# Attention stage of a transformer block: probabilities left unscaled, one query block's probabilities turned by way of DRAM, scores in plain fp32

## The chip, the cores and the metric

The kernel runs on one NeuronCore of one Trainium2 chip. The metric is the device time of one launch in microseconds; the number reported is the median of the runs.

## The reference

The input is 8192 tokens of width 512. It is layer-normalised to `xn`, and the output is `x + attention(xn) + feed_forward(xn)`. What matters here is the attention: 16 heads of width 32, in windows. A block of 128 queries sees three blocks of keys (its own and its two neighbours), masked to a distance of at most 128 tokens.

```python
qkv = (x @ Wqkv + bqkv)                      # q, k, v of 16 heads, 32 wide
scores = einsum('bhnqd,bhnkd->bhnqk', qb, kwin) * scale
attn   = softmax(where(mask, scores, -1e30)) # 128 queries x 384 keys
out    = einsum('bhnqk,bhnkd->bhnqd', attn, vwin)
return out @ Wout + bout
```

## The kernel before

There are two stages. The first, the feed-forward stage (up to about 1131 us), is not touched; it leaves the normalised input, transposed and split into a high and a low part, in DRAM. The second is `attention_stage`. Products whose operands are split run as three passes in the round fp32r form (high by high, low by high, high by low).

The attention stage has 128 steps `t` (`STEPS`). Step `t = 4 i + c` treats the two query blocks of token pair `i` (b = 0 and b = 1) for the four heads of channel group `c`. A query block of one head is a 128 x 384 tile of scores. Engines run their queues in the order in which the code writes them, and meet only at semaphores. Per step:

- TensorE (lines from 1064): `scores(t,0)`: three passes for four heads, 32 contraction rows for each head, one strip of the array for each (L1176). Then four quarters, each `turn_probs(t-1, 1, h)` (three 128 x 128 transposes, L1193) and a quarter of job A, which projects queries and keys for step t+2 (`run_a`, 24 matmuls of 256 columns, L1105). Then `scores(t,1)`, then `probs_times_values(t-1)` (L1217, plain fp32, four heads in four column strips of 32). Then four quarters, each `turn_probs(t, 0, h)` and a quarter of job B (`run_b`, 12 matmuls of 512 columns, L1114 for values or L1123 for the output projection).
- VectorE: `find_max` (L1006) adds the mask, scales and takes the maximum while it moves scores from PSUM to `probs`; `normalise` takes the reciprocal of the sums (L1017) and scales the probabilities of three heads of four (L1021); `qk_low` makes the low parts of queries and keys (L1034, L1038); `oT_low` (L1027) that of the product with the values; `add_out` (L1048) the output.
- ScalarE: `exp` (L928, with the sum and an accumulator read), `copy_pT` (L938, transposed probabilities from PSUM to SBUF), the high parts (L946, L954, L957), `take_v` (L921).
- GpSimd: the scaling of the fourth head (L888), key copies, `add_bias` (L899).
- SyncE's queue issues every DMA: `load_x` (L840), `load_part` (L846), `store_y` (L850), in one order written out by hand. It waits in that order too.

So before, all eight 128 x 384 tiles of a step are scaled and then turned by TensorE, 24 transposes in a step. The two `job_ps` banks are used in turn, and `wait_job_bank` holds a job until the job two before it was read out.

Of the kernel before, what the change touches and what calls it, by code (L numbers as in the profile page):

```python
# [22 lines left out]
P = 128  # L23
# [638 lines left out]
def attention_stage(nc, loaded, xT_dram, partial, out):  # L662
# [6 lines left out]
    VR = 6  # L669
    XR = 3  # L670

    ctx = ExitStack()
    with ctx:
# [18 lines left out]
        q_hi = sb("q_hi", [P, DC, 2, P], F32R)  # L692
        q_lo = sb("q_lo", [P, DC, 2, P], F32R)
        k_hi = sb("k_hi", [P, DC, 6, P], F32R)
        k_lo = sb("k_lo", [P, DC, 6, P], F32R)
# [5 lines left out]
        pT = wqkv_raw[:, 2:4, :].rearrange("p a (h w k) -> p (a h) w k", w=6, k=P)  # L701
        oT_hi = sb("oT_hi", [P, 2, DC, T], F32R)
        oT_lo = sb("oT_lo", [P, 2, DC, T], F32R)
# [13 lines left out]
        k0_hi, k0_done = sem("k0_hi"), sem("k0_done")  # L717
        qk_hi_done, qk_done = sem("qk_hi_done"), sem("qk_done")
# [6 lines left out]
        normalised, last_head_normalised = sem("normalised"), sem("last_head_normalised")  # L725
# [3 lines left out]
        oT_hi_done, oT_done = sem("oT_hi_done"), sem("oT_done")  # L729
# [40 lines left out]

        def job_a(t):
            return t + 2 if t + 2 < STEPS else None
# [19 lines left out]
        def job_release(n):  # L792

            t, k = divmod(n, 3)
            if k == 0:
                return (qk_done, job_a(t) + 1) if job_a(t) is not None else None
            if k == 1:
                return (oT_done, t) if 1 <= t <= STEPS else None
            b = job_b(t)
            if b is None:  # L800
                return None
            return (v_done, 2 * b[1] + b[2] + 2) if b[0] == "v" else (out_added, 2 * b[1] + b[2] + 1)

        def wait_job_bank(pe, n):
# [4 lines left out]
            if n >= 0:  # L809
                pe.wait_ge(*job_release(n))  # L810
            elif n % 2 == 0:
                pe.wait_ge(v_done, 2)
            else:
                pe.wait_ge(qk_done, 2)
# [17 lines left out]
        def _(sp):  # L832
# [14 lines left out]

            def store_y(i, b):
# [8 lines left out]
            for i in range(NT + 1):  # L857
                if 1 <= i:
                    for b in range(2):
                        store_y(i - 1, b)  # L860
                        if i < NT:
                            load_part(i, b)
                if i + XR - 1 < NT:
                    load_x(i + XR - 1)
            for b in range(2):
                sp.wait_ge(y_stored[b], 16 * NT)

        @block.gpsimd
        def _(pool):
# [13 lines left out]
            def normalise_last_head(t, b):  # L883
                i, _ = where(t)
                cols = window(i, b)
                u = b * HC + HC - 1
                pool.wait_ge(rcp_done, 2 * (2 * t + b) + 2)
                nc.gpsimd.tensor_scalar(probs[:, u, cols], probs[:, u, cols], sum_rcp[:, u:u + 1], None, ALU.mult  # L888
                                        ).then_inc(last_head_normalised, 1)

            def copy_keys(u):
                i, c = where(u)
                pool.wait_ge(qk_done, u + 1)
                nc.gpsimd.tensor_copy(k_hi[:, c, 0:2, :], k_hi[:, c, 4:6, :])
                nc.gpsimd.tensor_copy(k_lo[:, c, 0:2, :], k_lo[:, c, 4:6, :]).then_inc(keys_copied, 1)
# [7 lines left out]
            for t in range(STEPS + 3):  # L903
# [3 lines left out]
                if t < STEPS:  # L907
                    normalise_last_head(t, 0)
                if job_a(t) is not None and where(job_a(t))[0] % 2 == 0:
                    copy_keys(job_a(t))  # L910
                if t < STEPS:
                    normalise_last_head(t, 1)
# [3 lines left out]
        def _(act):  # L916
            def take_v(i, r, number, bank):
                act.wait_ge(job_filled, number)
                if i >= 2:
                    act.wait_ge(pv_done, 4 * i - 4)  # L920
# [10 lines left out]
            def copy_pT(t, b, h):  # L931
                i, _ = where(t)
                seen = blocks_seen(i, b)
                first = 3 * at(i, b)
                act.wait_ge(turned, 8 * t + b * HC + h + 1)
                if t >= 1:
                    act.wait_ge(pv_done, t)
                nc.scalar.copy(pT[:, h, first + seen.start:first + seen.stop, :].rearrange("p w t -> p (w t)"),  # L938
                               pT_ps[:, h % 2, seen.start * P:seen.stop * P]).then_inc(pT_done, 1)

            def oT_high(t):
                i, c = where(t)
                act.wait_ge(pv_done, t + 1)
                if i >= 2 and c == 0:
                    act.wait_ge(job_filled, B_NUMBER[4 * (i - 1) + 2])
                nc.scalar.copy(oT_hi[:, i % 2, c, :], job_ps[:, pv_bank(t), 0:T]).then_inc(oT_hi_done, 1)  # L946

            def qk_high(u, number, bank):
# [3 lines left out]
                if u >= DC:  # L952
                    act.wait_ge(scored, 2 * (u - DC) + 2)
                nc.scalar.activation(q_hi[:, c, :, :].rearrange("p b t -> p (b t)"), job_ps[:, bank, 0:T], ACT.Identity,  # L954
                                     bias=qk_bias[:, c:c + 1], scale=1.0)
                half = new_keys_at(i)
                nc.scalar.activation(k_hi[:, c, half:half + 2, :].rearrange("p b t -> p (b t)"),  # L957
                                     job_ps[:, bank, T:2 * T], ACT.Identity,
                                     bias=qk_bias[:, DC + c:DC + c + 1], scale=1.0).then_inc(qk_hi_done, 1)
# [9 lines left out]
            for c in range(DC):  # L969
                last = nc.scalar.activation(k_hi[:, c, keys_start(0) + 1, :], job_ps[:, 0, c * P:(c + 1) * P], ACT.Identity,  # L970
                                            bias=qk_bias[:, DC + c:DC + c + 1], scale=1.0)
            last.then_inc(k0_hi, 1)
            take_v(-1, 1, 2, 1)
            for u in range(2):
                qk_high(u, 3 + u, u)
            take_v(0, 0, 5, 0)
            for t in range(STEPS + 3):
# [3 lines left out]
                for h in range(HC):  # L981
                    if 1 <= t <= STEPS:
                        copy_pT(t - 1, 1, h)
                    if t < STEPS:
                        exp(t, 0, h)
                if job_a(t) is not None:
                    qk_high(job_a(t), A_NUMBER[t], a_bank(t))
                for h in range(HC):
                    if t < STEPS:
                        exp(t, 1, h)  # L990
                    if h == 0 and 1 <= t <= STEPS:
                        oT_high(t - 1)
                    if t < STEPS:
                        copy_pT(t, 0, h)

        @block.vector
        def _(dve):
            def find_max(t, b):
# [3 lines left out]
                if t >= 1:  # L1002
                    dve.wait_ge(turned, 8 * (t - 1) + HC * (b + 1))
# [6 lines left out]
            def normalise(t, b):  # L1010
                i, _ = where(t)
                cols = window(i, b)
                for pair in range(2):
                    first = b * HC + 2 * pair
                    heads = slice(first, first + 2)
                    dve.wait_ge(exped, 8 * t + first + 2)
                    nc.vector.reciprocal(sum_rcp[:, heads], prob_sum[:, heads]).then_inc(rcp_done, 1)  # L1017
                    dve.wait_ge(rcp_done, 2 * (2 * t + b) + pair + 1)
                    for u in range(first, first + 2):
                        if u % HC < HC - 1:  # L1020
                            nc.vector.tensor_scalar(probs[:, u, cols], probs[:, u, cols], sum_rcp[:, u:u + 1], None,  # L1021
                                                    ALU.mult).then_inc(normalised, 1)

            def oT_low(t):
                i, c = where(t)
                dve.wait_ge(oT_hi_done, t + 1)
                nc.vector.tensor_tensor(oT_lo[:, i % 2, c, :], job_ps[:, pv_bank(t), 0:T],  # L1027
                                        oT_hi[:, i % 2, c, :].bitcast(F32), ALU.subtract).then_inc(oT_done, 1)

            def qk_low(u, bank):  # L1030
                i, c = where(u)
                half = new_keys_at(i)
                dve.wait_ge(qk_hi_done, u + 1)
# [319 lines left out]
```

## Time and profile before

| | us |
|---|---|
| median of 3 runs | 2630.59 (2626.28 to 2631.04) |
| profiled execution | 2629.41, span 2627.6 |
| TensorE matmul busy | 2576.2 (98%) |
| ScalarE / VectorE / GpSimd busy | 1638.1 / 1592.0 / 631.8 |
| mean granted TensorE clock | 0.989 |
| HBM traffic | 97.43 MB read, 67.11 MB written |

The span is the time from the first to the last instruction; what a run takes beyond it (1.8 us here) lies around it. Busy shares are means over both stages. In the chain of waits each piece is work that nothing could have started earlier; its sum is the span.

### The profile page before, as it was taken

The page shows a single profiled execution, that of the slowest core. Times are in us where ns is not written, and L with a number is a line of the kernel's source. Part 1 is how long each engine was busy: PE and PEld are TensorE (multiplying, and loading weights), DVE is VectorE, ACT ScalarE, POOL GpSimd, SP SyncE. Part 2 cuts the span into 40 slices and gives each one's busy share as a digit, 9 for nine tenths or more (in the row PEclk, how much of TensorE's full clock was granted, in tenths as well). Part 3 has the DMA queues.
Part 4 walks back from the last instruction along what each step waited for, and adds up shares of the span by engine and source line. Part 5 has one row for each costly group of instructions (what it writes and reads, how often), then busy time and mean ns, then how long its engine had stood idle before and what let it go on. Part 6 is the DMA issues. An engine that isn't in the chain of part 4 may idle for free.

```text
span 2627.6 us, 55989 instructions
## 1 busy us (share of the span) xinstructions
PE 2576.2 (98%) x19728; PEld 2090.2 (80%) x19728; DVE 1592.0 (61%) x4779; ACT 1638.1 (62%) x4260; POOL 631.8 (24%) x595
## 2 busy tenths in 40 slices
PE   6999999999999999989999999999999999999998
PEld 4888888888888888868888888888888888888885
DVE  5444444444444444357777777777777777777775
ACT  6333333333333333358888888888888888888886
POOL 0011111111111111033333333333333333333332
PEclk7999999999999999999999999999999999999999
DMA  5422222222222222021121111112111111112110
GB/s 181 146 80 81 80 80 80 80 80 80 80 80 80 80 80 64 33 81 34 34 65 34 53 46 42 58 41 58 34 61 39 42 58 42 58 34 65 34 46 29
DMA packets 188361, 167.43 MB, mean 64 GB/s; under 512 B 11328, under 2 KB 143424, under 8 KB 187632
## 3 DMA queue, kind: packets, MB, share of 16 engines
q1 hardware_dynamic: 188000, 164.41, 20.2%
q8 instruction: 132, 2.16, 0.4%
q14 instruction: 85, 0.70, 0.1%
q0 software_dynamic: 144, 0.17, 0.0%
HBM read 97.43 MB, written 67.11 MB: 63 GB/s over the span
## 4 chain that ended last, share of the span: by engine, by line
PE 55%; ACT 1%; issue 0%; DVE 0%; POOL 0%; POOLq 0%; ACTq 0%
PE pT_ps L1193 14%; PE job_ps L1105 14%; PE score_ps L1176 7%; PE job_ps L1123 7%; PE job_ps L1217 7%; PE job_ps L1114 7%; ACT wqkv_raw L928 1%; ACT wqkv_raw L938 0%; PE job_ps L1237 0%; PE score_ps L1227 0%; DVE wqkv_raw L1006 0%; DVE k_lo L1038 0%; ACT q_hi L954 0%; ACT k_hi L957 0%; POOL wout_raw L899 0%
## 5 line engine op out<-in xcount | busy, mean ns | idle before, releaser
L928 ACT ACTIVATE wqkv_raw<-wqkv_raw,neg_max 128x384 f32<-128x384 f32 (+1 forms) x1024 | 633.3, 619 | 186.3 <-DVE neg_max L1006 181.5
L888 POOL TENSOR_SCALAR wqkv_raw<-wqkv_raw,sum_rcp 128x384 f32<-128x384 f32 (+1 forms) x256 | 372.9, 1457 | 960.1 <-DVE sum_rcp L1017 960.1
L494 ACT ACTIVATE relu<-up_ps,fc_scale 128x512 f32<-128x512 f32 x256 | 176.2, 688 | 656.2 <-PE up_ps L625 656.2
L938 ACT COPY wqkv_raw<-pT_ps 128x384 f32<-128x384 f32 (+1 forms) x1024 | 484.7, 474 | 74.4 <-PE pT_ps L1193 74.1
L1193 PE MATMUL pT_ps<-ident,wqkv_raw 128*128 128x128 f32 x3040 | 513.4, 277 | 8.1 <-ACT wqkv_raw L938 7.7
L1006 DVE CUSTOM_DVE_ANT_0 wqkv_raw<-score_ps,mask 128x384 f32<-128x384 f32 (+1 forms) x1024 | 503.5, 548 | 5.7 <-PE score_ps L1176 1.6
L568 DVE SCALAR_TENSOR_TENSOR sq<-up_ps,relu 128x512 f32<-128x512 f32 x256 | 177.0, 692 | 531.8 <-ACT relu L494 530.4
L1193 PEld LDWEIGHTS pT_ps<-ident,wqkv_raw 128*128 128x128 f32 x3040 | 360.0, 140 | 119.1 <-ACT wqkv_raw L938 42.6
L635 PE MATMUL down_ps<-proj_T,sq_hi 128*128 128x512 f32 x1024 | 408.9, 399 | 0.9 <-DVE sq_lo L551 0.9
L637 PE MATMUL down_ps<-proj_T,sq_lo 128*128 128x512 f32 x1024 | 404.3, 395 | 0.0
L621 PE MATMUL up_ps<-f_xT_hi,fc_T 128*128 128x512 f32 x1024 | 399.2, 390 | 1.4 <-DVE low L539 1.4
L623 PE MATMUL up_ps<-f_xT_lo,fc_T 128*128 128x512 f32 x1024 | 399.2, 390 | 0.0
L1105 PE MATMUL job_ps<-xT_hi,wqkv_hi 128*128 128x256 f32 x1024 | 329.0, 321 | 0.1
L1021 DVE TENSOR_SCALAR wqkv_raw<-wqkv_raw,sum_rcp 128x384 f32<-128x384 f32 (+1 forms) x768 | 298.2, 416 | 17.9
L1017 DVE RECIPROCAL sum_rcp<-prob_sum 128x2 f32<-128x2 f32 x512 | 85.0, 166 | 354.5 <-ACT wqkv_raw L928 354.0
L1105 PE MATMUL job_ps<-xT_hi,wqkv_lo 128*128 128x256 f32 x1024 | 287.9, 281 | 0.0
L1105 PE MATMUL job_ps<-xT_lo,wqkv_hi 128*128 128x256 f32 x1024 | 287.8, 281 | 0.0
L454 POOL TENSOR_TENSOR f_y<-f_y,part_in 128x512 f32<-128x512 f32 x64 | 86.9, 1389 | 665.1 <-DVE f_y L559 665.1
L635 PEld LDWEIGHTS down_ps<-proj_T,sq_hi 128*128 128x128 f32 x1024 | 193.4, 189 | 43.9 <-DVE sq_lo L551 2.2
L621 PEld LDWEIGHTS up_ps<-f_xT_hi,fc_T 128*128 128x128 f32 x1024 | 192.3, 188 | 44.0 <-DVE low L539 2.2
L637 PEld LDWEIGHTS down_ps<-proj_T,sq_lo 128*128 128x128 f32 x1024 | 193.0, 188 | 43.0
L623 PEld LDWEIGHTS up_ps<-f_xT_lo,fc_T 128*128 128x128 f32 x1024 | 192.3, 188 | 42.5
(126 smaller groups left out, 4228.2 us busy)
## 6 DMA issues: line engine op xcount, KB each, us to landing
xT_hi<-xT SPq DMA_DIRECT2D x65, 256.0 KB, 3.8
xT_lo<-xT SPq DMA_DIRECT2D x65, 256.0 KB, 4.5
f_x_in<-in_L_attn_x SPq DMA_DIRECT2D x64, 256.0 KB, 3.2
xT<-f_xT_hi SPq DMA_DIRECT2D x64, 256.0 KB, 2.6
xT<-f_xT_lo SPq DMA_DIRECT2D x64, 256.0 KB, 2.8
part_in<-in_L_attn_x SPq DMA_DIRECT2D x64, 256.0 KB, 3.4
partial<-f_y SPq DMA_DIRECT2D x64, 256.0 KB, 2.0
wout_raw<-partial SPq DMA_DIRECT2D x64, 256.0 KB, 2.8
```

The source lines that it names most:

```text
L621: nc.tensor.matmul(up_ps[:, s % 2, :], fc_T[:, k, cols], xT_hi[:, par, k, :], start=(k == 0), stop=False)
L623: nc.tensor.matmul(up_ps[:, s % 2, :], fc_T[:, k, cols], xT_lo[:, par, k, :], start=False, stop=False)
L635: nc.tensor.matmul(down_ps[:, b, :], sq_hi[:, s % 2, t], proj_T[:, s, :], start=(s == 0), stop=False)
L637: last = nc.tensor.matmul(down_ps[:, b, :], sq_lo[:, s % 2, t], proj_T[:, s, :], start=False, stop=(s == FB - 1))
L888: nc.gpsimd.tensor_scalar(probs[:, u, cols], probs[:, u, cols], sum_rcp[:, u:u + 1], None, ALU.mult).then_inc(last_head_normalised, 1)
L928: nc.scalar.activation(probs[:, u, cols], probs[:, u, cols], ACT.Exp, bias=neg_max[:, u:u + 1], scale=-1.0, accum_out=prob_sum[:, u:u + 1] ...
L938: nc.scalar.copy(pT[:, h, first + seen.start:first + seen.stop, :].rearrange("p w t -> p (w t)"), pT_ps[:, h % 2, seen.start * P:seen.stop ...
L1006: nc.vector.tensor_tensor_reduce(out=probs[:, u, cols], in0=score_ps[:, h, cols], in1=mask[:, cols], scale=-SCORE_SCALE, scalar=3e38, op0= ...
L1021: nc.vector.tensor_scalar(probs[:, u, cols], probs[:, u, cols], sum_rcp[:, u:u + 1], None, ALU.mult).then_inc(normalised, 1)
L1105: last = nc.tensor.matmul(job_ps[:, bank, is_k * T:(is_k + 1) * T], w[:, k, col:col + P], tokens, start=(m == 0), stop=(m == PASSES * DC - 1))
L1114: last = nc.tensor.matmul(job_ps[:, bank, :], a[:, k, x_slot(i) + r, :], w[:, k, 2 * D:3 * D], start=(n == 0), stop=(n == PASSES * DC - 1))
L1193: last = nc.tensor.transpose(pT_ps[:, h % 2, w * P:(w + 1) * P], probs[:, u, w * P:(w + 1) * P], ident[:, :])
```

## The change

Four things change together, all in the attention stage.

1. Probabilities stay unscaled. `inverse_sums` takes one reciprocal for four heads; GpSimd widens it to 32 columns for each head (`rcp_wide`); TensorE turns it (one transpose more in two of the four `turn_probs`), and `scale_oT` multiplies the product with the values by it, once for a step.
2. The probabilities of query block b = 0 are no longer turned by TensorE. VectorE turns 32 x 32 squares (`turn_blocks`), one DMA writes the four heads to DRAM (`move_blocks_out`, 786,432 bytes in pieces of 512 bytes) and four DMAs read them back in turned order (`move_blocks_in`). `probs_times_values` waits for that.
3. The product with the values is issued as six blocks of 128 columns for each head, instead of two of 256 and two of 128.
4. Scores are one plain fp32 product for each head, instead of three fp32r passes. Queries and keys are no longer split: `take_q` (ScalarE) and `take_k` (VectorE).

The values ring goes from 6 to 5 slots; the split product ring becomes `OR = 6` slots of one step. The bank of a product is released by `oT_scaled`, earlier by `oT_done`. The diff, cut to its core ("..." marks what is left out):

```diff
+        queries = sb("queries", [P, DC, 2, P], F32)
+        keys = sb("keys", [P, DC, 6, P], F32)
+        blocks = wqkv_raw[:, 3, :].rearrange("p (a w h t) -> p a w h t", w=3, h=HC, t=DH)
+        pT_moved = wqkv_raw[:, 2, :].rearrange("p (w q h t) -> p w q h t", q=STRIPS, h=HC, t=DH)
+        pT = sb("pT", [P, HC, 4, P], F32)
+        rcp_wide = sb("rcp_wide", [P, 2, HC, DH], F32)
...
             if k == 1:
-                return (oT_done, t) if 1 <= t <= STEPS else None
+                return (oT_scaled, t) if 1 <= t <= STEPS else None
...
+            def move_blocks_out(t):
+                sp.wait_ge(blocks_turned, HC * (t + 1))
+                if first == 0:
+                    sp.dma_start(moved.rearrange("a w p x -> p (a w) x"),
+                                 blocks.rearrange("p a w h t -> p (a w) (h t)")).then_inc(blocks_out, 16)
...
+            def move_blocks_in(t):
+                sp.wait_ge(blocks_out, 16 * transfers_out(t + 1))
+                if t >= 1:
+                    sp.wait_ge(pv_done, t)
+                for a in range(STRIPS):
+                    moved = turned_dram[t % 2 * STRIPS + a, first:3, :, :].rearrange("w (q j) x -> j (w q) x", j=DH)
+                    sp.dma_start(pT_moved[a * DH:(a + 1) * DH, first:3, :, :, :].rearrange("j w q h t -> j (w q) (h t)"),
+                                 moved).then_inc(blocks_moved, 16)
...
+            for t in range(STEPS + DC):
+                i, c = where(t)
+                if t < STEPS:
+                    move_blocks_out(t)
+                    move_blocks_in(t)
+                if c == 1 and i + XR - 1 < NT:
                     load_x(i + XR - 1)
+                if c >= 2 and i >= 1:
+                    store_y(i - 1, c - 2)
+                    if i < NT:
+                        load_part(i, c - 2)
...
                 for h in range(HC):
                     if 1 <= t <= STEPS:
-                        copy_pT(t - 1, 1, h)
+                        copy_pT(t - 1, h)
                     if t < STEPS:
                         exp(t, 0, h)
-                    qk_high(job_a(t), A_NUMBER[t], a_bank(t))
+                    take_q(job_a(t), A_NUMBER[t], a_bank(t))
                 for h in range(HC):
                         exp(t, 1, h)
-                    if h == 0 and 1 <= t <= STEPS:
-                        oT_high(t - 1)
-                    if t < STEPS:
-                        copy_pT(t, 0, h)
+                if 1 <= t <= STEPS:
+                    oT_high(t - 1)
...
+            def turn_blocks(t, u):
+                dve.wait_ge(exped, 8 * t + u + 1)
+                if u == 0 and t >= 1:
+                    dve.wait_ge(blocks_out, 16 * transfers_out(t))
+                nc.vector.transpose(blocks[:, :, seen.start:seen.stop, u, :].rearrange("p a w t -> p w a t"),
+                                    probs[:, u, seen.start * P:seen.stop * P].rearrange("p (w a t) -> p w a t", a=STRIPS, t=DH)
+                                    ).then_inc(blocks_turned, 1)
+
+            def scale_oT(t):
+                dve.wait_ge(pv_done, t + 1)
+                if t >= 1:
+                    dve.wait_ge(oT_done, t)
+                nc.vector.tensor_tensor(oT.rearrange("p (b t) -> p b t", t=P),
+                                        job_ps[:, pv_bank(t), 0:T].rearrange("p (b t) -> p b t", t=P),
+                                        pT[:, HC - 2:HC, 3, :], ALU.mult).then_inc(oT_scaled, 1)
...
                     find_max(t, 0)
-                    normalise(t, 0)
+                    for u in range(HC):
+                        turn_blocks(t, u)
+                    inverse_sums(t, 0)
-                    qk_low(job_a(t), a_bank(t))
+                    take_k(job_a(t), a_bank(t))
                     find_max(t, 1)
+                    scale_oT(t - 1)
+                    inverse_sums(t, 1)
                     oT_low(t - 1)
-                    normalise(t, 1)
...
+                for h in range(HC):
+                    rows = slice(h * DH, (h + 1) * DH)
+                    last = nc.tensor.matmul(score_ps[:, h, cols], queries[rows, c, place, :],
+                                            keys[rows, c, first + seen.start:first + seen.stop, :],
+                                            start=True, stop=True, tile_position=(h * DH, 0))
...
+                if h >= HC - 2:
+                    pe.wait_ge(rcp_widened, 2 * t + 2)
+                    last = nc.tensor.transpose(pT_ps[:, h % 2, 3 * P:4 * P],
+                                               rcp_wide[:, at(i, place), :, :].rearrange("p h t -> p (h t)"), ident[:, :])
...
+                pe.wait_ge(blocks_moved, 16 * STRIPS * (t + 1))
+                pe.wait_ge(pT_done, HC * (t + 1))
+                for b in range(2):
...
+                    for w in seen:
...
+                            p = pT[:, h, w, :].rearrange("p (q t) -> p q t", t=DH) if b else pT_moved[:, w, :, h, :]
+                            last = nc.tensor.matmul(out_, values[:, blk % VR, head * DH:(head + 1) * DH], p,
+                                                    start=(w == seen.start), stop=(w == seen.stop - 1),
+                                                    tile_position=(0, h * DH))
...
                 for part in range(QUARTERS):
-                    if t < STEPS:
-                        turn_probs(t, 0, part)
                     run_b(t, part)
```

## Rows read from the trace of the kernel before

**Rows 1.** The page, part 1: busy time and share of the span, by engine.
```profile
PE 2576.2 (98%) x19728; PEld 2090.2 (80%) x19728; DVE 1592.0 (61%) x4779; ACT 1638.1 (62%) x4260; POOL 631.8 (24%) x595
```
**Rows 2.** The page, part 4: the chain that ended last, by engine and line.
```profile
PE 55%; ACT 1%; issue 0%; DVE 0%; POOL 0%; POOLq 0%; ACTq 0%
PE pT_ps L1193 14%; PE job_ps L1105 14%; PE score_ps L1176 7%; PE job_ps L1123 7%; PE job_ps L1217 7%; PE job_ps L1114 7%; ACT wqkv_raw L928 1%; ACT wqkv_raw L938 0%; PE job_ps L1237 0%; PE score_ps L1227 0%; DVE wqkv_raw L1006 0%; DVE k_lo L1038 0%; ACT q_hi L954 0%; ACT k_hi L957 0%; POOL wout_raw L899 0%
```
**Rows 3.** The chain in order of time, one step: start, us, what.
```profile
1801.84 0.73 PE score_ps L1176 x9
1802.57 0.48 PE pT_ps L1193 x3
1803.05 0.71 PE job_ps L1105 x6
1803.76 0.33 PE pT_ps L1193 x3
...
1807.59 1.44 PE job_ps L1217 x32
...
1809.51 0.70 PE job_ps L1123 x3
...
1813.28 0.73 PE score_ps L1176 x12
```
**Rows 4.** Windows: interior of the attention stage, and its end.
```profile
core 0: us, PE busy (x) PEld busy (x) DVE busy (x) ACT busy (x) POOL busy (x), PEclk, DMA share, GB/s
1180.00:2600.00 1420.00, 1415.62 (x14332) 1152.10 (x14324) 1038.48 (x3671) 1166.63 (x3420) 482.78 (x430) 1.00 0.15 46
2600.00:2627.60 27.60, 17.83 (x120) 11.58 (x112) 8.55 (x31) 9.09 (x30) 6.67 (x6) 0.80 0.11 39
```
**Rows 5.** Timeline of TensorE: product with the values, then scores. Start, us, form, count.
```profile
1807.53 1.07 PE L1217 MATMUL job_ps<-wqkv_raw,values 128*32 128x256 f32 x16
1808.41 0.62 PE L1217 MATMUL job_ps<-wqkv_raw,values 128*32 128x128 f32 x16
...
1813.49 0.35 PE L1176 MATMUL score_ps<-k_hi,q_lo 32*128 32x384 f32 x4
1813.66 0.35 PE L1176 MATMUL score_ps<-k_lo,q_hi 32*128 32x384 f32 x4
```
**Rows 6.** Timeline of ScalarE and VectorE, middle of the same step.
```profile
1807.10 0.19 ACT L928 ACTIVATION_READ_ACCUMULATOR wqkv_raw<-wqkv_raw,neg_max 128x1 f32 x1
...
1807.32 0.17 DVE L1017 RECIPROCAL sum_rcp<-prob_sum 128x2 f32<-128x2 f32 x1 [1.13 <-ACT wqkv_raw L928]
1807.52 0.42 DVE L1021 TENSOR_SCALAR wqkv_raw<-wqkv_raw,sum_rcp 128x384 f32<-128x384 f32 x1
...
1808.84 0.55 DVE L1006 CUSTOM_DVE_ANT_0 wqkv_raw<-score_ps,mask 128x384 f32<-128x384 f32 x1
```
**Rows 7.** DMA issues: count, KB each, median us from issue to landing.
```profile
xT<-f_xT_hi SPq DMA_DIRECT2D x64, 256.0 KB, 2.6
...
wout_raw<-partial SPq DMA_DIRECT2D x64, 256.0 KB, 2.8
...
fc_in<-in_L_ffn_w_fc SPq DMA_DIRECT2D x16, 256.0 KB, 5.9
...
wqkv_raw<-in_L_attn_Wqkv SPq DMA_DIRECT2D x4, 768.0 KB, 8.2
```
**Rows 8.** SyncE's queue, timeline: start and us of the issue itself.
```profile
505.53 0.54 SPq L411 DMA_DIRECT2D xT<-f_xT_hi  x1
...
1827.84 0.34 SPq L850 DMA_DIRECT2D out<-wout_raw  x1
...
1828.71 1.22 SPq L840 DMA_DIRECT2D xT_hi<-xT  x2
```
**Rows 9.** Windows: a stretch in which four xT loads run (columns as in rows 4).
```profile
1828.70:1833.50 4.80, 4.80 (x64) 3.68 (x63) 3.64 (x13) 3.38 (x11) 1.46 (x1) 1.00 1.00 273
```
**Rows 10.** Timeline, last step: end of its fourth exponential, and its product with the values.
```profile
2604.01 0.20 ACT L928 ACTIVATION_READ_ACCUMULATOR wqkv_raw<-wqkv_raw,neg_max 128x1 f32 x1
...
2611.45 2.40 PE job_ps L1217 x24
```

More of the change, by code:

```diff
@@ L724, in attention_stage @@
         rcp_done = sem("rcp_done")
-        normalised, last_head_normalised = sem("normalised"), sem("last_head_normalised")
+        rcp_widened = sem("rcp_widened")
+        blocks_turned, blocks_out, blocks_moved = sem("blocks_turned"), sem("blocks_out"), sem("blocks_moved")
         turned = sem("turned")
@@ L795, in job_release @@
             if k == 0:
[L796 removed]
+                return (k_done, job_a(t) + 1) if job_a(t) is not None else None
             if k == 1:
[L798 removed]
+                return (oT_scaled, t) if 1 <= t <= STEPS else None
             b = job_b(t)
@@ L881, in _, with widen_inverse_sums @@
             pool.wait_ge(bias_added, 1)
[L883 to L889, printed above, removed]
+            def widen_inverse_sums(t, b):
+                pool.wait_ge(rcp_done, 2 * t + b + 1)
+                if t >= 1:
+                    pool.wait_ge(turned, HC * t)
+                heads = slice(b * HC, (b + 1) * HC)
+                nc.gpsimd.tensor_copy(rcp_wide[:, b, :, :], sum_rcp[:, heads].unsqueeze(2).to_broadcast([P, HC, DH])
+                                      ).then_inc(rcp_widened, 1)
             def copy_keys(u):
                 i, c = where(u)
-                pool.wait_ge(qk_done, u + 1)
-                nc.gpsimd.tensor_copy(k_hi[:, c, 0:2, :], k_hi[:, c, 4:6, :])
-                nc.gpsimd.tensor_copy(k_lo[:, c, 0:2, :], k_lo[:, c, 4:6, :]).then_inc(keys_copied, 1)
+                pool.wait_ge(k_done, u + 1)
+                nc.gpsimd.tensor_copy(keys[:, c, 0:2, :], keys[:, c, 4:6, :]).then_inc(keys_copied, 1)
             def add_bias(i, b):
@@ L953, in qk_high @@
                     act.wait_ge(scored, 2 * (u - DC) + 2)
[L954 to L959, printed above, removed]
+                nc.scalar.activation(queries[:, c, :, :].rearrange("p b t -> p (b t)"), job_ps[:, bank, 0:T],
+                                     ACT.Identity, bias=qk_bias[:, c:c + 1], scale=1.0).then_inc(q_done, 1)
             act.wait_ge(wqkv_here, 64)
@@ L1001, in find_max @@
                 dve.wait_ge(scored, 2 * t + b + 1)
-                if t >= 1:
-                    dve.wait_ge(turned, 8 * (t - 1) + HC * (b + 1))
+                if t >= 1 and b == 0:
+                    dve.wait_ge(blocks_turned, HC * t)
+                if t >= 1 and b == 1:
+                    dve.wait_ge(turned, HC * t)
                 for h in range(HC):
@@ L1008, in find_max, with inverse_sums @@
                                                    accum_out=neg_max[:, u:u + 1]).then_inc(maxed, 1)
-            def normalise(t, b):
-                i, _ = where(t)
[L1012 to L1022, printed above, removed]
+            def inverse_sums(t, b):
+                heads = slice(b * HC, (b + 1) * HC)
+                dve.wait_ge(exped, 8 * t + (b + 1) * HC)
+                if t >= 1:
+                    dve.wait_ge(rcp_widened, 2 * (t - 1) + b + 1)
+                nc.vector.reciprocal(sum_rcp[:, heads], prob_sum[:, heads]).then_inc(rcp_done, 1)
```

172 lines of the change are left out of this document (73 added, 99 removed).

## The prediction

> **What bounds the kernel now.** I read the busy line first: TensorE's matmuls cover 98% of the span and no other engine passes 62% [rows 1]. Busy is not yet the bound, so next comes the chain that ended last: 55% of the span is TensorE inside the attention stage, six lines of it, and other engines have 1% or less [rows 2]. Then the same chain in order of time [rows 3]: scores start at 1801.84 and again, one step later, at 1813.28. A step is 11.44 us, and it is TensorE work end to end: two scores of 0.73, two groups of transposes at 0.48 (the first after a change of tiling) and six of 0.33, four quarters of job A at 0.71, four of job B at 0.70, the product with the values at 1.44; the sum is 1.46 + 2.94 + 2.84 + 2.80 + 1.44 = 11.48. In the interior TensorE is idle 4.4 of 1420 us and its clock is full [rows 4]. So an edit pays here by what it takes from TensorE's queue, until another chain is longer.
>
> **What goes from TensorE.** `turn_probs(t,0,h)` goes: four groups of three transposes. The first stands behind the product with the values and shows 0.48; of that 0.15 is the change of tiling, which the first job B matmul will now pay. So 4 x 0.33 = 1.32 us go for each step [rows 3].
>
> **What comes to TensorE.** The turned reciprocals: two transposes more, one of 0.33 / 3 = 0.11 each, 0.22 us [rows 3].
> Scores: a pass of four heads, 384 columns, starts every 0.17 us (1813.49, 1813.66) [rows 5]: one column a cycle at full clock, with the four heads side by side. Plain fp32 does not appear in row strips before. In column strips it does: the trace holds two matmuls for each one written (32 for 16), and four groups of four with 256 columns take (1.07 - 0.42) / 3 = 0.22 us each, 0.42 being the length of one; that is two cycles a column and matmul [rows 5]. For 384 columns that makes 2 x 0.32 = 0.64 us against 3 x 0.16 = 0.48, or +0.16 for each of two calls: +0.32. Bounds: 0 (eight matmuls in place of twelve, if the two halves ran at the fp32r pace), and, if heads in plain fp32 ran one after the other, 4 x 0.64 - 0.48 = +2.1 each, +4.2 for a step. I take +0.32, since the nearest row runs side by side.
> Product with the values: the columns stay 768 for each head and half; groups of 128 columns start every (0.62 - 0.27) / 3 = 0.117 us, 0.27 being one matmul's length, so half of the 0.217 of a 256 group [rows 5]. Twelve such groups are 1.40, against 4 x 0.217 + 4 x 0.117 = 1.34: +0.06. The moving operand of b = 0 is now in four runs of 32; bounds 0 and +0.6 (were a group held by the eight instructions in it at half again the pace). I take +0.06.
> TensorE's step is then 11.44 - 1.32 + 0.22 + 0.32 + 0.06 = 10.72 us.
>
> **The new chain.** The probabilities of b = 0 must leave VectorE, go to DRAM, come back, and be there for the product, which stands one step later. Counted from the start of scores(t,0): the fourth exponential of b = 0 ends at 1807.10 + 0.19 - 1801.77 = 5.52 now [rows 6] (the timeline has scores start 0.07 ahead of the chain). It is paced by the turns of step t-1, so later scores (0.16), two wider turns (0.22) and a wider copy (0.1) put it at 6.00. VectorE then starts within 0.05 (1807.29 to 1807.32), and I give the 32 x 32 turn of 128 x 384 the 0.42 of a tensor_scalar of that size [rows 6]; bounds 0.42 and 0.84 (twice, for output in runs of 32). Blocks turned: 6.5.
> Out, 786,432 bytes: a 256 KB store in pieces of 512 bytes lands after 2.6 us [rows 7]. With the engines full 273 GB/s were moved [rows 9], so 0.96 of that is data and 1.64 fixed. 768 KB: 1.64 + 2.88 = 4.5. Its issue is longer: 0.34 for 128 pieces, 0.54 for 512 [rows 8], by that slope 1.07 for 1536; half of the 0.5 more gives 4.8. Back: 1.9 fixed (2.8 of a 256 KB load less 0.9 [rows 7]) + 2.88 = 4.8; the four issues of about 0.55 each lie under the data [rows 8]. I take 4.8 + 4.8, and 0.3 for three semaphores: the tile is there at 6.5 + 9.9 = 16.4. Upper bound from the row of 768 KB, 8.2 each way [rows 7] (loads queued behind ten others): 16.4 + 6.8 = 23.2. Lower: 4.5 + 4.5, 15.8.
> TensorE reaches the product at 10.72 + (1807.53 - 1801.77 = 5.76 now, + 0.32 + 0.22 = 6.30) = 17.0. So the chain is hidden, with 0.6 us to spare: the smallest margin in the plan. Being late by d costs d / 2 for each step, because the stall moves the next step's start as well (lag two steps).
> The Trainium skill ("DMA: Bandwidth & Descriptors", section on the anatomy of one DMA) fits a DMA of the software path as about 2.0 us + bytes / 436e3, which would be 3.8 each way, and a margin of 2.6 instead of 0.6. The trace's 273 GB/s with 512-byte pieces speaks against its data rate; no run here shows 768 KB alone. The sum does not use it.
>
> **The queues.** SyncE's: in a step it issues one out, four in, then at c = 1 four xT loads (0.61 each), at c = 2, 3 a store and a load. It sits in `move_blocks_in` until the out has landed, at 11.4, issues until 13.6, then the xT loads until 16.1; the next out is due at 10.72 + 6.5 = 17.2. Their 1 MB at 273 GB/s takes 3.8 us, to about 18.5, when the next out's packets begin (17.2 + 1.2): touching in one step of four. DMA load: 1.57 MB more for each step over 273 GB/s is 5.8 us, with 2 MB for four steps 1.8 more: 7.6 of 10.7, so no throughput bound. I allow 0.05 us a step for touches and instruction loads.
> VectorE: turns 1.7, find_max 8 x 0.5, one key move 0.4 for two lows of 0.48, one scaling 0.4 and two reciprocals 0.35, six scalings of 0.4 gone: about 7.7 of 10.7, 8.4 before. In order: turns end 6.5, key move by 7.1, four maxima by 9.1, `scale_oT` by 9.5; job B needs the key move by 7.8 and step t+1 the maxima by 10.7. ScalarE: four copies go, one activation goes; its last exponential of b = 1 ends near 10.3, under the next turn at 11.9. GpSimd loses 2 x 1.46 and gains two small copies; rcp_widened is due at 10.3 + 0.6, needed by the third turn at 10.72 + 3.0. None of these is late.
>
> **The end.** Steps 126 and 127 have no job A, so nothing covers the round trip. The fourth exponential ends at 2604.21 and the product starts at 2611.45, 7.24 later [rows 10]; it will need 0.5 + 9.9 = 10.4: +3.2. `scale_oT` adds 0.4 to the last links, and TensorE idles more just where its clock is already 0.80 [rows 4]: 1.5 more. Together +5.
>
> **Sum.** 126 interior steps x (11.44 - 10.77) = 84.4 saved, 5 given back: 2629.4 - 79.4 = 2550.0. The profiled execution lies 1.2 below the median, so 2551.
>
> **Rivals.**
> (A) The round trip sets the step, and the kernel becomes slower. Place: the wait for blocks_moved ahead of L1217. From d = 0.6 late on it bites; each microsecond past the margin costs 0.5 a step, so the 0.68 that the step was to gain are gone 1.4 past it, when out and in take 9.6 + 0.6 + 1.4 = 11.6 together. For: each of the two has DRAM on one side, no 768 KB store in 512-byte pieces is in the trace, the weight loads took 8.2 [rows 7]. Against: those stood in a full queue, and 5.9 for 256 KB there [rows 7] is more than twice what the same size takes later. At 6.5 + 6.5 the step is 10.72 + (3.4 - 0.6) / 2 = 12.12: 126 x 0.68 = 86 us more and 5 at the end, 2721. Chance 0.20.
> (B) The round trip is late, but less: 5.3 + 5.3 is 0.4 past the margin, a step of 10.92 and 2570; 5.6 + 5.6 makes 11.0 and 2582, and so on to 2610; an engine order that VectorE's turn lengthens comes out here too (0.84 for 0.42 makes the chain 0.42 longer). Chance 0.22.
> The Trainium skill ("VectorE: DVE Perf Modes", section on the three transpose paths) gives 311 ns for 128 x 128 in bf16; three of those are an estimated 0.93 us for a head, and the chain 0.5 longer, hardly past the margin: about 2555. No row here shows the operation.
> (C) Products cost more on TensorE: the strided operand at its bound, +0.6 - 0.06 = 0.54 a step: 2619. Chance 0.05.
> (D) Plain fp32 in row strips runs head after head: +3.9 a step, 3040. Against: fp32 in column strips does not. Chance 0.03.
> (E) My forecast, TensorE bound with short waits, 2530 to 2570: chance 0.50.
>
> **How the numbers follow.** Faster: E, B and C together, less a little of B that comes out level: 0.75. A measurement of this kernel tells 0.2% (5 us) from no change; that band holds 0.03. Slower: A and D, 0.22. The range takes E, B, C and the near half of A: 2520 to 2680.
>
> **What would show it.** Right: steps of 10.7 to 10.8, transposes 14 instead of 24 in a step, a score call near 0.89, the product near 1.5, and no idle time ahead of L1217's successor that a DMA ends. Wrong in the DMA term: TensorE idle once a step ahead of the product, released by pT_moved's DMA. Wrong in VectorE's: a turn above 0.8, or idle time of the scores released by VectorE.

## The result, and the profile after

The changed kernel takes 2589.31 us in the median (2587.77 to 2590.46, 4 runs), against 2630.47 us before on the same chip: a ratio of 0.9847, 95% interval 0.9829 to 0.9864. It is 41 us faster; 80 were forecast. The profiled execution has a span of 2587.3 us.

Page of after, parts 1 and 6 (busy time; DMA issues with count, KB each, median us to landing):

```profile
PE 2482.6 (96%) x19488; PEld 1984.0 (77%) x19488; DVE 1530.9 (59%) x4263; ACT 1450.9 (56%) x3620; POOL 317.4 (12%) x531
...
turned_blocks<-wqkv_raw SPq DMA_DIRECT2D x124, 768.0 KB, 4.7
wqkv_raw<-turned_blocks SPq DMA_DIRECT2D x496, 192.0 KB, 3.6
xT_hi<-xT SPq DMA_DIRECT2D x65, 256.0 KB, 4.8
```

And part 4, the chain that ended last, by engine:

```profile
PE 47%; DMA 4%; issue 2%; ACT 1%; SPq 1%; DVE 0%; POOLq 0%; POOL 0%; ACTq 0%
```

Against [rows 1] TensorE's busy time fell by 93.6 us, more than twice what the kernel gained. Against [rows 2] the chain has a stretch that was not there: DMA 4%. So part of what TensorE gave up came back as waiting for the blocks. The window over the interior says how much (columns as in [rows 4]):

```profile
1180.00:2560.00 1380.00, 1324.78 (x14086) 1045.96 (x14086) 984.36 (x3184) 986.07 (x2809) 178.19 (x372) 1.00 0.73 189
```

TensorE is idle 55 of 1380 us, where it was idle 4.4 of 1420 [rows 4], and the DMA engines are busy 0.73 of the time against 0.15. The stretch of the chain in which it happens: a stall, the product that waited, and then the round trip of the next block (start, us, what):

```profile
1806.64 0.80 issue
1807.44 1.52 PE job_ps L1248 x48
1808.96 2.98 PE job_ps L1149 x12
1811.95 0.86 PE score_ps L1208 x8
1812.80 0.48 PE pT_ps L1221 x3
1813.28 0.71 PE job_ps L1140 x6
...
1817.14 0.71 ACT wqkv_raw L964 x2
...
1817.88 0.59 DVE wqkv_raw L1055
...
1818.49 5.26 DMA turned_blocks<-wqkv_raw
1823.77 0.32 SPq L878
...
1825.16 3.80 DMA wqkv_raw<-turned_blocks
1828.95 0.25 issue
1829.20 1.52 PE job_ps L1248 x48
```

The first row is TensorE idle for 0.80 us ahead of the product with the values. It carries no releaser's name. The last rows show what such a wait is made of: the turn on VectorE 0.59, the out transfer 5.26, four issues on SyncE's queue (the last starts 1.4 after the first), the last in transfer 3.80. The timeline of SyncE's queue tells why some steps stall and others do not (start and us of the issues):

```profile
1702.27 1.84 SPq L878 DMA_DIRECT2D wqkv_raw<-turned_blocks  x4
1704.16 1.22 SPq L849 DMA_DIRECT2D xT_hi<-xT  x2
1705.42 1.30 SPq L849 DMA_DIRECT2D xT_lo<-xT  x2
1707.55 0.38 SPq L863 DMA_DIRECT2D turned_blocks<-wqkv_raw  x1
1714.47 1.85 SPq L878 DMA_DIRECT2D wqkv_raw<-turned_blocks  x4
...
1741.45 0.38 SPq L863 DMA_DIRECT2D turned_blocks<-wqkv_raw  x1
1745.58 2.14 SPq L878 DMA_DIRECT2D wqkv_raw<-turned_blocks  x4
```

From the out transfer to the first in transfer it is 4.1 us in one step in which nothing stands ahead (1741.45 to 1745.58) and 6.9 us behind four xT loads (1707.55 to 1714.47). These two are near the ends of a scatter: over steps 8 to 119 the out transfer takes 5.70 us in the mean for c = 2, behind the xT loads, and 4.53, 4.54 and 4.69 for c = 0, 1 and 3, with single ones from 4.1 to 7.1. The interval from `scores(t,0)` to `scores(t+1,0)`, over the same 112 steps of the timeline by c, is 10.72, 10.94, 10.93 and 11.85 us for c = 0, 1, 2, 3; the step with c = 3 holds the product whose out transfer stood behind the xT loads. The mean is 11.11 (11.09 over steps 4 to 123), where an undisturbed step has 10.64 to 10.69.

### The profile page after: what moved, and what is told of

It is laid out like the page before. It is cut to its first block, busy times and chain, and to the rows that moved or that the text cites. A ratio compares the mean times of both kernels' runs of the same rounds, so it can differ in the third digit from the quotient of the medians.

```text
span 2587.3 us, 54843 instructions
## 1 busy us (share of the span) xinstructions
PE 2482.6 (96%) x19488; PEld 1984.0 (77%) x19488; DVE 1530.9 (59%) x4263; ACT 1450.9 (56%) x3620; POOL 317.4 (12%) x531
## 4 chain that ended last, share of the span: by engine, by line
PE 47%; DMA 4%; issue 2%; ACT 1%; SPq 1%; DVE 0%; POOLq 0%; POOL 0%; ACTq 0%
PE job_ps L1140 12%; PE job_ps L1158 7%; PE score_ps L1208 7%; PE job_ps L1248 7%; PE pT_ps L1221 6%; PE job_ps L1149 6%; DMA turned_blocks<-wqkv_raw 2%; DMA wqkv_raw<-turned_blocks 2%; ACT wqkv_raw L964 1%; PE pT_ps L1226 1%; SPq L878 1%; DVE wqkv_raw L1055 0%; ACT pT L974 0%; PE job_ps L1268 0%; PE score_ps L1258 0%
## 5 line engine op out<-in xcount | busy, mean ns | idle before, releaser
L964 ACT ACTIVATE wqkv_raw<-wqkv_raw,neg_max 128x384 f32<-128x384 f32 (+1 forms) x1024 | 622.1, 608 | 152.4 <-DVE neg_max L1038 152.4
L1055 DVE STREAM_TRANSPOSE wqkv_raw<-wqkv_raw 128x384 f32<-128x384 f32 (+1 forms) x512 | 292.7, 573 | 172.4 <-ACT wqkv_raw L964 158.1
L974 ACT COPY pT<-pT_ps 128x384 f32<-128x384 f32 (+2 forms) x512 | 272.3, 532 | 183.7 <-PE pT_ps L1221 174.5
L1221 PE MATMUL pT_ps<-ident,wqkv_raw 128*128 128x128 f32 x1520 | 256.9, 278 | 1.3 <-ACT pT L974 1.3
L1208 PE MATMUL score_ps<-keys,queries 32*128 32x384 f32 (+1 forms) x2048 | 235.8, 530 | 3.3 <-DVE neg_max L1038 2.6
L1221 PEld LDWEIGHTS pT_ps<-ident,wqkv_raw 128*128 128x128 f32 x1520 | 174.2, 141 | 71.7 <-issue 69.0
L924 POOL COPY rcp_wide<-sum_rcp 128x128 f32<-128x128 f32 x256 | 75.5, 295 | 1147.1 <-DVE sum_rcp L1047 1147.1
L1140 PEld LDWEIGHTS job_ps<-xT_lo,wqkv_hi 128*128 128x128 f32 x1024 | 195.5, 191 | 0.0
```

Source lines behind the costliest of these rows:

```text
L964: nc.scalar.activation(probs[:, u, cols], probs[:, u, cols], ACT.Exp, bias=neg_max[:, u:u + 1], scale=-1.0, accum_out=prob_sum[:, u:u + 1] ...
L974: nc.scalar.copy(pT[:, h, seen.start:last, :].rearrange("p w t -> p (w t)"), pT_ps[:, h % 2, seen.start * P:last * P]).then_inc(pT_done, 1)
L1055: nc.vector.transpose(blocks[:, :, seen.start:seen.stop, u, :].rearrange("p a w t -> p w a t"), probs[:, u, seen.start * P:seen.stop * P]. ...
L1140: last = nc.tensor.matmul(job_ps[:, bank, is_k * T:(is_k + 1) * T], w[:, k, col:col + P], tokens, start=(m == 0), stop=(m == PASSES * DC - 1))
L1208: last = nc.tensor.matmul(score_ps[:, h, cols], queries[rows, c, place, :], keys[rows, c, first + seen.start:first + seen.stop, :], start= ...
L1221: last = nc.tensor.transpose(pT_ps[:, h % 2, w * P:(w + 1) * P], probs[:, u, w * P:(w + 1) * P], ident[:, :])
```

## Experiments

Theory 1: TensorE's own work fell as the sum said, and the round trip holds it, mostly where an out transfer queues behind the xT loads. Rival theories: the longer order on VectorE and ScalarE also holds TensorE; or the round trip is late in itself, or the DMA engines have too much to move, wherever the xT loads stand.

**No transfers.** The five DMAs of a step go, and the waits on them.

```diff
-                    move_blocks_out(t)
-                    move_blocks_in(t)
+                    sp.wait_ge(blocks_turned, HC * (t + 1))
...
-                if u == 0 and t >= 1:
-                    dve.wait_ge(blocks_out, 16 * transfers_out(t))
...
-                pe.wait_ge(blocks_moved, 16 * STRIPS * (t + 1))
```

> Leaves out the five DMAs that move the turned blocks and the waits on them; the product for b = 0 reads stale data, all other instructions stay. Theory (the round trip is the only thing that holds TensorE in the changed kernel): steps of 10.68 us as TensorE's own work adds up in the trace of after, against 11.09 on average, so 120 x 0.41 = 49 us less, and the 5 us at the end come back: about 2536 us. Rival (the longer order on VectorE and ScalarE also holds TensorE): steps stay above 10.8, 2550 us or more.

Measured 2527.18 us, 0.961 of before (0.9594 to 0.9627). Its interior window:

```profile
1180.00:2460.00 1280.00, 1278.72 (x13678) 1013.99 (x13667) 947.88 (x3069) 952.90 (x2709) 171.00 (x359) 1.00 0.17 50
```

TensorE is idle 1.3 of 1280 us and a step is 10.66. So VectorE, ScalarE and GpSimd hold next to nothing; the whole distance of 62 us between this kernel and the changed one is the round trip's, the end included. The guess was missed by 9 us: the stall was 11.09 - 10.66 = 0.43 a step rather than 0.41 (52 us over 120 steps, not 49), and from the scores of step 124 to the end it is 54.3 us against 63.9, so the round trip costs 9.6 there and not 5.

**No xT loads in the steady state.**

```diff
-                if c == 1 and i + XR - 1 < NT:
-                    load_x(i + XR - 1)
+                if c == 1 and i + XR - 1 == XR - 1:
+                    load_x(XR - 1)
...
```

> The changed kernel with the xT loads of the steady state left out (later steps project stale tokens); the blocks still go by way of DRAM. Theory 1 (queue order: the out transfer of the step with c = 2 stands behind 1 MB of xT loads): the mean interval from scores to scores of that place falls from 11.85 us to about 10.8, 31 x 1.05 = 33 us less, about 2556 us. Theory 2 (the round trip is too long in itself, wherever the xT loads stand): the other steps, 10.72 to 10.94, show what is left, and the gain is under 10 us.

Measured 2565.83 us, 0.9759 (0.9743 to 0.9776). The step of the 11.85 fell to 11.00, but the others did not fall to 10.66: for c = 0, 1 and 2 they are 10.96, 10.84 and 10.72. Some 24 us of the 62 are the xT loads', by their place or their bytes, and a stall of 0.21 us a step is left that neither theory had in full.

**xT loads spread**, one in each step.

```diff
...
-                if c == 1 and i + XR - 1 < NT:
-                    load_x(i + XR - 1)
+                if c >= 1 and i + XR - 1 < NT:
+                    load_x_piece(i + XR - 1, c - 1)
+                if c == 0 and 1 <= i and i + XR - 2 < NT:
+                    load_x_piece(i + XR - 2, 3)
```

> The changed kernel with the four xT loads of a pair issued one in each step, behind that step's blocks, instead of four behind the blocks of the step with c = 1. Same bytes, same number of DMAs. Theory 1 (queue order): no out transfer finds more than 256 KB ahead of it, the 11.85 us place falls to about 10.9, 2555 to 2565 us. Theory 2 (the DMA engines have too much to move, 0.73 of them busy): nothing changes, 2585 to 2592 us, only that the stalls spread evenly.

Measured 2575.72 us, 0.9794 (0.9778 to 0.981): between the two. The long step moved to c = 0 (11.28), whose product has its out transfer behind a store, a load and an xT load; the mean step is 11.00.

**xT loads ahead of the out transfer.**

```diff
                 sp.wait_ge(blocks_turned, HC * (t + 1))
+                if t % DC == 2 and i + XR - 1 < NT:
+                    load_x(i + XR - 1)
...
-                if c == 1 and i + XR - 1 < NT:
-                    load_x(i + XR - 1)
```

> The changed kernel with the four xT loads issued directly ahead of the out transfer of the step with c = 2 (after the blocks are turned). Same bytes. Theory 1 (queue order): that out transfer is issued 2.5 us later and waits for 1 MB (3.8 us); now it is late by about 2 us for this reason, so 2 to 4 us more for each of 31 pairs: 2650 to 2710 us. Theory 2 (throughput): no change, 2585 to 2595 us.

Measured 2753.58 us, 1.0478 (1.0454 to 1.0501): with the same bytes 164 us slower than the changed kernel. The place of four DMAs in the queue decides between gain and loss. It overshoots the expectation. One row of its TensorE timeline, the product that waited:

```profile
1832.84 0.44 PE L1248 MATMUL job_ps<-wqkv_raw,values 128*32 128x128 f32 x4 [4.87 <-issue]
```

the same place in its chain:

```profile
1827.97 4.87 issue
1832.84 2.79 PE job_ps L1248 x48
1835.63 4.27 PE job_ps L1149 x12
```

and two windows, its interior and the 3.4 us from that product on:

```profile
1180.00:2600.00 1420.00, 1273.88 (x12984) 1009.55 (x12980) 890.44 (x2908) 907.38 (x2569) 162.07 (x341) 0.95 0.64 170
1832.80:1836.20 3.40, 3.36 (x50) 2.91 (x51) 0.51 (x2) 0.05 (x1) 0.00 (x0) 0.50 0.79 243
```

TensorE was idle 146 us in the interior, and its mean granted clock was 0.95, where the other interior windows shown here have 1.00. Right after the wait it is 0.50, the lower of the two levels (1.2 instead of 2.4 GHz): the product takes 2.79 us instead of 1.45, and job B 4.27 instead of 2.99. The step with c = 3 is 17.5 us in the mean: 10.6 of work, 4.9 of waiting for the product, and some 2.0 more that go with the lower clock. Over 31 pairs that is about 60 us, an estimate, more than the 44 by which the forecast was overshot. So these waits cost more than their idle time, and the 164 us are not all queue.

**One part alone: plain fp32 scores in the kernel before.**

```diff
-                for pass_ in range(PASSES):
-                    q = q_lo if pass_ == 1 else q_hi
-                    keys = k_lo if pass_ == 2 else k_hi
-                    for h in range(HC):
+                for h in range(HC):
...
-                                                start=(pass_ == 0), stop=(pass_ == PASSES - 1),
+                                                start=True, stop=True,
...
```

> The kernel before with one part of the change alone: queries and keys unsplit, scores one plain fp32 product for each head. Theory (TensorE bound, and a score call goes from 0.73 to 0.86 us as in the trace of after): 256 calls x 0.13 = 33 us more, about 2663 us. Rival (the two low parts and the high part of the keys that go from VectorE and ScalarE shorten something): 2640 us or less.

Measured 2660.73 us, 1.0116 (1.0099 to 1.0133). A step is 11.72 instead of 11.44. This part costs 31 us and buys nothing in time.

**The DRAM way undone.** The changed kernel with b = 0 turned on TensorE.

```diff
...
                 for part in range(QUARTERS):
+                    if t < STEPS:
+                        turn_probs(t, 0, part)
                     run_b(t, part)
```

> The changed kernel with the blocks of b = 0 turned by TensorE again, in job B's quarters as before, instead of by way of DRAM; everything else as changed. Theory (each group of three transposes is 0.33 us of TensorE, four of them): steps of 10.66 + 1.32 = 11.98 us and no round trip: 128 x 0.54 = 69 us over the kernel before, about 2699 us. Rival (the removal of the scaling from VectorE and GpSimd brings something by itself): 2660 us or less.

Measured 2687.99 us, 1.0225 (1.0207 to 1.0242). Its chain, one step (start, us, what):

```profile
1796.45 0.86 PE score_ps L1167 x8
1797.31 1.45 PE job_ps L1206 x48
1798.76 0.48 PE pT_ps L1180 x3
...
1808.40 0.86 PE score_ps L1167 x8
```

A step is 11.95 us. Together with the run above: unscaled probabilities, the turned reciprocals and the smaller products cost 27 us (2687.99 - 2660.73), about what 128 pairs of turned reciprocals add up to (0.22 each, 28 us). The DRAM way is worth 161 us where nothing waits for it (2687.99 - 2527.18), of which the round trip took 62 back. The parts add up to the whole: 31 + 27 - 161 + 62 = -41 us. Whether the DRAM way would also do with scaled probabilities was not tried.

**Strips.** If the round trip is near its limit everywhere, a shorter one should pay more than a better place for the xT loads. An in transfer reads one strip of 32 rows, and needs only that strip's out transfer.

```diff
...
+                for a in range(STRIPS):
+                    sp.dma_start(moved[a, first:3, :, :].rearrange("w p x -> p w x"),
+                                 blocks[:, a, first:3, :, :].rearrange("p w h t -> p w (h t)")).then_inc(strip_out[a], 16)
...
-                sp.wait_ge(blocks_out, 16 * transfers_out(t + 1))
...
                 for a in range(STRIPS):
+                    sp.wait_ge(strip_out[a], 16 * (t + 1))
...
```

> The changed kernel with the out transfer cut in four, one DMA and one semaphore for each strip; each of the four in transfers waits only for its own strip. Same bytes, same 512-byte pieces. Theory (the round trip is late by one to three microseconds in the steps that stall): the in transfers are issued some 2 us earlier, so most of the 0.43 us of stall goes: steps of 10.7 to 10.8, 2535 to 2550 us. Rival (the engines are short of throughput, as the remaining 0.21 and 0.34 us of stall without the xT loads and with them spread suggest): over 2570 us.

Measured 2533.49 us, 0.9638 (0.9622 to 0.9654), 56 us under the changed kernel. Its interior window, and SyncE's queue for one step:

```profile
1180.00:2500.00 1320.00, 1315.07 (x14056) 1042.37 (x14057) 976.91 (x3165) 980.73 (x2795) 176.13 (x370) 1.00 0.79 196
```

```profile
1794.66 2.55 SPq L864 DMA_DIRECT2D turned_blocks<-wqkv_raw  x4
1797.32 2.58 SPq L875 DMA_DIRECT2D wqkv_raw<-turned_blocks  x4
```

Here the first in transfer is issued 2.7 us after the first out transfer. Over steps 8 to 119 it is 2.8 us in the mean where the changed kernel has 4.9, and the last in transfer lands 15.45 us after `scores(t,0)` instead of 17.25; TensorE asks for it at 16.9. TensorE is idle 4.9 of 1320 us; a step is 10.66, all four places within 10.64 to 10.69. The DMA engines are busier than in the changed kernel (0.79): they had no lack of throughput at 0.73.

**Strips, in transfers wait for all four.** What helped, the overlap or the cutting? The edit is shown against Strips.

```diff
                 for a in range(STRIPS):
                     sp.wait_ge(strip_out[a], 16 * (t + 1))
+                for a in range(STRIPS):
                     moved = turned_dram[t % 2 * STRIPS + a, first:3, :, :].rearrange("w (q j) x -> j (w q) x", j=DH)
```

> As strips, with one thing taken back: all four out transfers must have landed before the first in transfer is issued. Theory 1 (what helped was the overlap of out and in): the round trip is as long as with one out transfer, 2580 to 2600 us. Theory 2 (what helped was the cutting itself, four DMAs of 192 KB landing sooner than one of 768 KB): 2530 to 2550 us.

Measured 2597.16 us, 0.987 (0.9853 to 0.9886). The gain is gone: it was the overlap. Beside the changed kernel it is even 8 us slower, perhaps for the four issues in place of one; the intervals of the two ratios overlap a little, so this is weakly shown.

**Strips, other DMAs placed evenly.** Two xT loads at c = 0 and two at c = 1, a store and a load at c = 2 and c = 3.

```diff
...
                 if c == 1 and i + XR - 1 < NT:
-                    load_x(i + XR - 1)
+                    load_x_piece(i + XR - 1, 0)
+                    load_x_piece(i + XR - 1, 1)
+                if c == 0 and 1 <= i and i + XR - 2 < NT:
+                    load_x_piece(i + XR - 2, 2)
+                    load_x_piece(i + XR - 2, 3)
```

> As strips, and besides the other DMAs evenly placed: two of 256 KB in each step (two xT loads at c = 0 and at c = 1, a store and a load at c = 2 and at c = 3). Theory: no stall is left but the one at the end, steps of 10.68, about 2533 us. Rival (throughput): no better than strips.

Measured 2533.65 us, 0.9638 (0.9622 to 0.9654): no better than strips. Once the round trip has room, moving the xT loads to this place changes nothing.

**Strips, with the scores back in fp32r.** The parts that pay, without the one that does not: the edit is that of the fp32 scores above, reversed.

```diff
-                for h in range(HC):
+                for pass_ in range(PASSES):
+                    q = q_lo if pass_ == 1 else q_hi
+                    keys = k_lo if pass_ == 2 else k_hi
+                    for h in range(HC):
...
```

> As strips, with the scores back in three fp32r passes over split queries and keys. Theory (parts add up, since TensorE is the bound again): 256 calls x 0.13 = 33 us less than strips (2533), about 2501 us. Rival (the two low parts on VectorE and the high part on ScalarE make find_max, the exponentials or the bank of job A late, or the step is now shorter than the round trip allows): 2515 us or more.

Measured 2521.83 us, 0.9579 (0.9562 to 0.9596): the fastest version, 109 us under the kernel before and 67 under the changed one, but 12 us gained on strips and not the 33 expected. A step is 10.49 to 10.55 in the mean by c, against 10.66 for strips and 10.40 hoped for. Two of its waits from 1200 to 2480 us (who waited for whom: us in total, times, longest; PEld is the weight load):

```profile
PEld job_ps L1174 <- DVE k_lo L1085: 18.2, 61, 0.3
PEld job_ps L1165 <- DVE k_lo L1085: 17.9, 58, 0.5
```

and a piece of its chain, in the slowest step with c = 3:

```profile
1822.92 0.73 PE score_ps L1227 x8
1823.64 1.21 issue
1824.85 1.52 PE job_ps L1268 x48
```

The score calls do fall to 0.73. But in nearly every step job B waits for the key's low part on VectorE, 0.3 us in the mean, to load its first weights (L1165 projects values, L1174 the output). Weight loads overlap matmuls, so only a part of it shows: the step is 0.09 to 0.15 longer than hoped for, about 16 us over 120 steps. The round trip plainly shows again in only one of the steps 8 to 119 (11.66 us, the piece above). Another 6 us were lost up to step 4 (its scores at 1196.70 in place of 1190.79). Part of that is the clock:

```profile
1170.00:1192.00 22.00, 17.70 (x213) 16.11 (x216) 13.87 (x52) 15.87 (x49) 1.92 (x6) 0.84 0.51 144
```

The granted clock is 0.84 there, where strips have 1.00, and some quarters of job A take 1.28 us instead of 0.71. TensorE had waited there for VectorE and ScalarE. The kernel before has the same difference: its first four steps take 41.4 us, and 38.1 with plain fp32 scores. The rival was right, in its number and in the bank of job A; its round trip counts for little.

## Why the prediction was right in sign and only half right in size

- **What bounds the kernel**: right. What was taken from TensorE's queue or given to it moved the time by nearly that amount, until another wait took over.
- **TensorE's step, 10.72 us**: right. It is 10.66 without transfers. By terms: a score call 0.86, predicted 0.89; so plain fp32 runs its four heads side by side in row strips, and rival D is out. The product 1.45 for 1.50, so C is out. Four groups of transposes: 11.95 - 10.66 = 1.29 for 1.32. The turned reciprocal 0.11 each, as said.
- **The round trip**: the step that failed, and in it the way back above all. The prediction had the tile there 0.6 us before TensorE asks for it, and allowed 0.05 us a step for touches. Over steps 8 to 119, in us after `scores(t,0)`:

  | | planned | measured, mean (range) |
  |---|---|---|
  | fourth exponential ends | 6.00 | 5.97 |
  | blocks turned | 6.5 | 6.58 |
  | the out transfer, issue to landing | 4.8 | 4.86 (4.1 to 7.1) |
  | the way back, first issue to last landing | 4.8 | 5.75 (5.2 to 7.2) |
  | tile is there | 16.4 | 17.25 (16.0 to 19.8) |
  | TensorE could start the product | 17.0 | 16.9 |

  A turn takes 0.58 us where 0.42 was planned, but the blocks are turned almost on time. The out transfer is right in the mean, but 5.70 where the xT loads stand ahead. The way back is 0.95 longer than planned, and 0.7 to 1.1 longer in each of the four places: the last issue comes 1.4 us after the first, and its transfer then takes 4.2 in the median (3.6 is the median of all four), so the issues do not lie under the data as planned. The margin is -0.3 us in the mean instead of +0.6, and the scatter does the rest, since a tile that is early gives nothing back.
- **Touches**: the prediction saw that the xT loads' data would end about when the next out transfer's began, called it touching in one step of four, and priced it at almost nothing. Without the xT loads 24 of the 62 us go. The rest is the way back and its scatter: without them the tile still lands at 16.9 in the mean, just when it is needed. The store and load ahead of the outs of c = 0 and c = 3 show little: 4.53 and 4.69, against 4.54 for c = 1 with none ahead. What makes single transfers scatter from 4.1 to 7.1 us is open.
- **The sum with what was measured**: the mean stall was 0.43 us a step where the plan had 0.05, 126 x 0.38 = 48 us; with the step 0.06 shorter than planned (8 us) that is 2551 + 48 - 8 = 2591, against 2589 measured.
- **Rival B** (2570 to 2610, chance 0.22) is what came, in mechanism and size. Out and in took 4.86 + 5.75 = 10.6 us, its first case (5.3 + 5.3), for which it gave steps of 10.92; with the scatter they are 11.09. Its second case has a slip: by the prediction's own rule 5.6 + 5.6 makes steps of 11.22 and about 2608 us, not 11.0 and 2582. The stated range of 2520 to 2680 held because it took in B; the forecast itself, 2551, was 38 us too low, since the sum had no spread for its tightest margin.
- **The Trainium skill's fit** ("DMA: Bandwidth & Descriptors", anatomy of one DMA), which is for the software path, gives an estimated 3.8 us for each way. The trace, on SyncE's queue with 512-byte pieces, disagrees: 4.1 at the least for 768 KB to DRAM, and 3.6 in the median already for 192 KB back. By these estimates no stall would have been there.
- **The Trainium skill's 311 ns** for a 128 x 128 turn ("VectorE: DVE Perf Modes", the three transpose paths) is for bf16. Taken three times it gives an estimated 0.93 for a head, the trace has 0.58, between that and the tensor_scalar's 0.42.
- **The lag**: that lateness counts half in the steady state (0.5 us a step for 1 late) was not tested by itself, but the trace shows its mechanism. After the stall of c = 2, 1.07 us in the mean, the tile of c = 3 lands at 17.07, which would be 0.2 too late in an undisturbed step; the product finds it there all the same and starts at 18.17, because the stall has moved it too.
- **The end**: the number is right, by luck. From scores of step 126 to the end it is 38.0 us before and 43.2 after, 5.2 for a predicted 5. But without transfers it is 35.7: the round trip costs 7.5 there, not the 3.2 that were planned, and without it the stretch is 2.3 shorter than before, which the plan did not count. From its fourth exponential to its product the last step takes 11.8 us, planned 10.4.
- **Why A did not come**: out and in together took 10.6 us in the mean, short of the 11.6 at which the gain is gone. With c = 2, behind the xT loads, they took just 11.6, but that is one step of four. The run with the xT loads ahead of the out transfer shows how close it was: it is rival A brought about by the order of the queue.

## What to carry to other kernels

When work is moved off the bounding engine and onto a round trip by DMA, sum two things: what the engine gives up, and the margin of the round trip in its worst queue position, not in its mean; the engine's idle time comes from the steps in which the margin is negative, and steps with room give nothing back (here a mean margin of -0.3 us became a stall of 0.43 a step). Here the round trip was shortened best by cutting it where its second half needs only a part of the first, with one semaphore for each part (56 us); spreading the transfers in its way brought 14. And time each part of a bundled change alone: here one of four parts cost 31 us under cover of the gain.

## What was not expected of the hardware

A VectorE turn of 32 x 32 squares over 128 x 384 fp32 takes 0.577 us in the mean, 1.4 times a tensor_scalar of that size (0.42, [rows 6]). The issue of a DMA on SyncE's queue does not grow with its pieces as [rows 8] suggested: 1536 pieces of 512 bytes are issued in 0.38 us, less than 512 pieces of xT stores (0.54). And the kernel with waits of 4.9 us on TensorE in one step of four had a mean granted clock of 0.95 over its interior. The changed kernel, whose waits go up to 2.6 us, had 1.00, but it fell once as well:

```profile
1853.00:1856.40 3.40, 3.40 (x51) 2.83 (x43) 1.15 (x7) 2.06 (x7) 0.30 (x1) 0.50 0.65 189
```

The product there takes 2.61 us instead of 1.52.
